# An attention loop of 16 chunks: x loaded as soon as x1 is made, y's high half taken before the second exponentials, x1's low half on GpSimd, and 50 constant products in the tail

## The reference

```
x = x + attention(cond(x, type))        # cond: shared + typed gated FFN, mixed by a gate
x = x + ffn(cond2(x, type))             # cond2: 3 shared + 2 typed FFNs, gated; ffn: router + top-2 of 8 experts
```

```
q, k, v = x @ Wq.T + bq, x @ Wk.T + bk, x @ Wv.T + bv
scores  = einsum('bhqd,bhkd->bhqk', q, k) / sqrt(16), masked above the diagonal
out     = softmax(scores) @ v @ Wo.T + bo
```

## Time and profile before

| what | value |
|---|---|
| time, median of 3 runs | 2447.77 us (2443.02 to 2448.24) |
| the profiled execution's own time | 2434.09 us |
| its span | 2432.5 us |
| PE busy | 2328.6 us, 96% of the span, 18946 matmuls |
| DVE busy | 1164.1 us, 48% |
| ACT busy | 1067.4 us, 44% |
| POOL busy | 294.1 us, 12% |
| attention stage, in the trace | from 573.6 us (constant products ahead of it) to 846.45 us (first L785 of es[0]) |

### The profile page before, as it was taken

How to read it: one execution, slowest core, us unless ns; L and a number is a source line. 1 busy time by engine, 2 the same in 40 slices (tenths; PEclk the granted TensorE clock), 3 DMA queues, 4 the chain that set the end, 5 groups by cost and what they waited for, 6 DMA issues and landing times.

```text
span 2432.5 us, 51603 instructions
## 1 busy us (share of the span) xinstructions
PE 2328.6 (96%) x18946; PEld 1516.3 (62%) x18965; DVE 1164.1 (48%) x2341; ACT 1067.4 (44%) x2049; POOL 294.1 (12%) x466
## 2 busy tenths in 40 slices
PE   5999999997999799999999999999999999989997
PEld 2444588885878544444444788888544444457886
DVE  5554355444888543233232444445344444444444
ACT  3553355442666443233232344433344454446662
POOL 0000000002433000000000111111000000004556
PEclk9999999998999899999999999999999999999999
DMA  3231011001334222021010233343111111002434
GB/s 122 88 100 55 27 53 52 35 14 53 84 91 92 63 104 78 26 78 61 27 61 26 92 117 108 107 140 106 57 38 50 34 35 34 35 35 70 130 96 124
DMA packets 165292, 170.22 MB, mean 70 GB/s; under 512 B 98932, under 2 KB 143348, under 8 KB 156164
## 3 DMA queue, kind: packets, MB, share of 16 engines
q1 hardware_dynamic: 139300, 80.35, 11.3%
q0 software_dynamic: 20720, 72.47, 8.8%
q10 hardware_dynamic: 5104, 15.12, 2.0%
HBM read 107.57 MB, written 50.86 MB: 65 GB/s over the span
## 4 chain that ended last, share of the span: by engine, by line
PE 85%; ACT 4%; SPq 3%; DVE 3%; issue 2%; DMA 2%; POOL 1%; DVEq 0%; POOLq 0%; ACTq 0%
PE ps L767 31%; PE ps L785 25%; PE ps L1042 14%; PE ps L1161 4%; PE ps L1173 4%; PE ps L1031 3%; SPq L508 1%; DMA arena<-in_x 1%; SPq L507 1%; ACT misc L1352 1%; ACT arena L1351 1%; SPq L603 1%; PE ps L1056 1%; PE ps L870 0%; DVE xh L1980 0%
## 5 line engine op out<-in xcount | busy, mean ns | idle before, releaser
L767 PE MATMUL ps<-xh,arena 128*128 (+1 forms) x5376 | 892.7, 308 | 18.4 <-DVE xh L1606 10.2
L785 PE MATMUL ps<-misc,arena 128*128 128x256 f16 (+2 forms) x4128 | 716.1, 309 | 13.8 <-DVE misc L1797 8.0
L767 PEld LDWEIGHTS ps<-xh,arena 128*128 (+1 forms) x5376 | 515.9, 98 | 292.0 <-issue 27.4
L785 PEld LDWEIGHTS ps<-misc,arena 128*128 (+1 forms) x4128 | 393.7, 98 | 231.7 <-issue 12.9
L1801 DVE SCALAR_TENSOR_TENSOR misc<-ps,misc 128x256 f16<-128x256 f32 (+1 forms) x464 | 248.1, 535 | 492.9 <-ACT misc L1273 491.1
L1273 ACT ACTIVATE misc<-ps 128x256 f16<-128x256 f32 (+1 forms) x464 | 218.5, 471 | 525.6 <-PE ps L767 525.6
L1042 PE MATMUL ps<-arena 128*128 128x512 f16 x1536 | 337.2, 379 | 0.0
L1042 PEld LDWEIGHTS ps<-arena 128*128 128x128 f16 x1536 | 148.0, 98 | 172.8
L2059 DVE TENSOR_TENSOR arena<-misc,arena 128x512 f16<-128x512 f32 x128 | 88.6, 692 | 228.5 <-ACT arena L1412 228.3
L1795 DVE TENSOR_TENSOR arena<-ps,misc 128x256 f32<-128x256 f32 (+1 forms) x200 | 101.8, 509 | 146.8 <-ACT misc L1269 146.0
L1411 ACT ACTIVATE misc<-ps,bias 128x512 f32<-128x512 f32 x128 | 87.7, 685 | 173.0 <-PE ps L1042 162.8
(11 more groups left out here) (284 smaller groups left out, 2110.0 us busy)
## 6 DMA issues: line engine op xcount, KB each, us to landing
wstage<-in_m_w POOLq DMA_DIRECT2D x16, 1024.0 KB, 5.9
parts_d<-misc POOLq DMA_DIRECT2D x64, 256.0 KB, 2.5
arena<-src_d SPq DMA_DIRECT2D x64, 256.0 KB, 3.8
src_d<-misc SPq DMA_DIRECT2D x24, 512.0 KB, 3.1
arena<-parts_d ACTq DMA_DIRECT2D x12, 1024.0 KB, 8.2
wstage<-in_c_wi POOLq DMA_DIRECT2D x6, 1024.0 KB, 5.7
wstage<-in_r_w POOLq DMA_DIRECT2D x5, 1024.0 KB, 5.3
cshare_d<-misc SPq DMA_DIRECT2D x8, 512.0 KB, 3.1
```

The costliest lines, as they stand in the source:

```text
L767: last = mm(ps[:, bank, col + c0:col + c0 + width], weight(off, half, g, wp, k * F + f * 128), xh[:, xp, k, ds(start, width)], start=(k == ...
L785: last = mm(ps[:, 4 + 2 * half + m, c0:c0 + width], weight(off, half, 2 if p.gated else 1, wp, f * D + m * 128), hid[:, st % 4, hp, c0:c0 ...
```

## The change

Four edits in the attention and one in the tail:

1. ACT calls `y_high(i + 2)` after the copy of the denominators and ahead of `exponentials(i, 1)`, instead of last in the turn.
2. ACT writes x1 scaled by SX in float32 into a new buffer `x1_scaled` (a part of `misc` that the attention leaves free), and then x1's high part as before.
3. POOL, not DVE, makes x1's low part (`x1_low`), as x1_scaled - high part, last in its turn. ACT waits for POOL's previous one before it overwrites `x1_scaled`, and once more behind the loop for the last one.
4. SP issues `xin_load(i - 1)` ahead of `x1_store(i - 2)`; the load now waits for x1 of the chunk before (`s["x1"]`), and the store waits for x1 and no more for its low part.
5. `keep_clock(2, 38)` becomes `keep_clock(2, 50)`.

```diff
+        x1_scaled = misc[:, 512:1024].rearrange("p (k n) -> p k n", k=KC)
...
-            for i in range(NA + 1):
-                if i >= 1:
+            def x1_low(c):
+                pool.wait_ge(s["x1_hi"], c + 1)
+                cols = ds(c * CH, CH)
+                nc.gpsimd.tensor_tensor(xh[:, 1, :, cols], x1_scaled, xh[:, 0, :, cols], ALU.subtract
+                                        ).then_inc(s["x1_lo"], 1)
+
+            for i in range(NA + 2):
+                if 1 <= i <= NA:
                     normalisers_wide(i - 1)
                 if i + 2 < NA:
                     y_sum(i + 2)
                     y_low(i + 2)
+                if i >= 2:
+                    x1_low(i - 2)
...
             def xin_load(c):
+                if c >= 1:
+                    sp.wait_ge(s["x1"], c)
                 for j in range(GB):
                     load_x(xin[:, :, j * S:(j + 1) * S], c * GB + j).then_inc(s["xin_in"], 16)
 
             def x1_store(c):
-                sp.wait_ge(s["x1_lo"], c + 1)
+                sp.wait_ge(s["x1"], c + 1)
...
+                if 0 <= i - 1 < NA:
+                    xin_load(i - 1)
                 if 0 <= i - 2:
                     x1_store(i - 2)
-                if 0 <= i - 1 < NA:
-                    xin_load(i - 1)
...
-            keep_clock(2, 38)
+            keep_clock(2, 50)
...
+                if i + 2 < NA:
+                    y_high(i + 2)
                 if 0 <= i < NA:
                     exponentials(i, 1)
                 if 0 <= i - 2 < NA:
                     act.wait_ge(s["x1"], i - 1)
+                    if i >= 3:
+                        act.wait_ge(s["x1_lo"], i - 2)
+                    fn(x1_scaled, x1, ACT.Copy, scale=SX)
                     fn(xh[:, 0, :, ds((i - 2) * CH, CH)], x1, ACT.Copy, scale=SX).then_inc(s["x1_hi"], 1)
-                if i + 2 < NA:
-                    y_high(i + 2)
-
+
+            act.wait_ge(s["x1_lo"], NA)
...
-                if 0 <= i - 2 < NA:
-                    dve.wait_ge(s["x1_hi"], i - 1)
-                    cols = ds((i - 2) * CH, CH)
-                    v.scalar_tensor_tensor(xh[:, 1, :, cols], x1, SX, xh[:, 0, :, cols],
-                                           ALU.mult, ALU.subtract).then_inc(s["x1_lo"], 1)
```

## The result

| | before | changed |
|---|---|---|
| time, median | 2448.01 us (2443.02 to 2449.20, 4 runs) | 2414.37 us (2409.48 to 2418.10, 4 runs) |
| ratio | | 0.9865 [0.9841, 0.9889] |
| profiled execution's own time | 2434.09 us | 2409.48 us |
| its span and mean granted clock | 2432.5 us, 0.989 | 2407.9 us, 0.991 |

The change makes the kernel 1.35% faster, 33.6 us between the medians. Between the two profiled executions, whose own times the sum was made from, the difference is 24.6 us where the sum said 20.3. So two things are to be found: what in the traces is larger than forecast, and why the medians lie 9 us further apart than the traces.

A forecast was written before the change was run, and what follows sets the result against it. PE and DVE were taken as nearly full, with PE's floor at 13.5 us per turn. Turns -13.4, loop's end -7.1 and constants +0.2 gave -20.3 us; against 2447.8 the forecast was 2427.5 us, range 2419.0 to 2438.5.

The forecast's parts named there:

- the sum: Whole kernel: turns -13.4, loop's end -7.1, constant products +0.2, together -20.3 us, from 2434.1 to 2413.8 for the profiled execution.
- the step from the sum to the forecast: Whole kernel: the profiled execution lay 13.7 us under the median; against 2447.8 us the forecast is 2427.5.
- They can keep no clock that was not kept: Tail: 12 more constant products before the combination keep no further clock and cost up to 0.3, +0.2 us.
- The turns: Attention's steady turns: from 14.53 to 13.5 us, 1.03 saved in each of 13 turns, -13.4 us.
- the floor: Attention: PE's own work per turn, 13.44 us measured in one turn and rounded up to 13.5.
- Rival B: Attention: DVE and POOL take turns at the shared ports; turns of 14.0, 2434 us, chance 0.16.
- rivals C and D: Attention: C, ACT becomes the ring, 2438.5 us, chance 0.11; D, SP's queue is slower, 2463 us, chance 0.03.
- DVE would fall to 11.5 per turn: Attention: without x1's low part DVE's list falls from 13.16 to 11.5 us at best, so it is no bound.
- The price that the prediction named for this case: Attention, y's high half moved: second exponentials end later; if exponentials began as late as now, PE would wait 0.4 us per turn.
- the longer path behind x1: Loop's end: one more copy and ACT's wait for POOL before es[0] give 1.9 us back.
- The loop's end: From the last turns to es[0]: last x1 9.0 us sooner, less 1.9, -7.1 us, from -3 to -10.
- its lower bound (the clock): Loop's end: -10 us if PE, at 1.2 GHz there, stays at 2.4 GHz.

The follow-up runs named there:

- experiment 2: The changed kernel with 38 constant products instead of 50: 2420.07 us, ratio 0.9918 to the kernel before.
- experiment 4: The kernel before with only SP's edit (load of x ahead of the store, both behind x1), 38 constants: 2426.18 us, ratio 0.9935.
- experiment 7: The kernel before with SP's edit and y's high half moved, x1's low part left on DVE, 38 constants: 2420.38 us, ratio 0.9916.
- experiment 6: The kernel before with only y's high half moved ahead of the second exponentials, 38 constants: 2447.06 us, ratio 1.0023.
- experiment 5: The changed kernel measured once more, no edit: 2416.03 us, ratio 0.9904 to the kernel before.
- experiment 3: The kernel before with 50 constant products instead of 38, nothing else: 2437.85 us, ratio 0.9991.
- experiment 8: The changed kernel without SP's edit (store waits for x1's low part, load behind it): 2462.23 us, ratio 1.0089 to the kernel before.
- experiment 11: The changed kernel with x1's low part left on DVE, 50 constants: 2415.34 us, ratio 0.9892 to the kernel before.
- experiment 10: The changed kernel with two buffers for x and constant products in PE's waits at the loop's end: 2409.13 us, ratio 0.9867 to the kernel before.

## Why the prediction was right or wrong

**The step that failed** is the one from the sum to the forecast: "Against 2447.8 the forecast is 2427.5". It took the 20.3 us from an execution of 2434.09 and moved them to the median of three runs, 13.7 us higher, as if the same offset would stand between the changed kernel's trace and its median. It did not: there the offset was 4.9 us (2409.48 to 2414.37). Of the 13.1 us by which the forecast missed, 8.8 are this difference of the offsets and 4.3 lie in the traces (24.6 against 20.3): the loop's end gave 1.1 more than forecast, the step behind it 1.6 and the first turns 1.6, and the sum had no term for the last two. The offset should have been a question: what in this kernel can differ by 10 us between two executions?

**One cause of the offset was a term of the sum**: "They can keep no clock that was not kept", +0.2 us. It was read from one execution, whose combination ran at 2.4 GHz behind an idle time of 2.34. In 31 of the 71 executions of the kernel before the mean clock was low; in the four traces of kernels with 38 constants where it was 0.985 or less, the combination had fallen to 1.2 GHz and cost 9.3 us more (experiments 2, 4, 7 and, with the same 10.40 behind 2.35 of idle time, 6). At that share the 12 constants are worth 31/71 x 9.3 = 4.1 us on the mean, less 0.3; with the 7.7 between the medians of the two heaps it is 3.4, less 0.3. Experiment 2 against 5 gives 2420.07 - 2416.03 = 4.0 us, but on two chips, and the direct comparison, experiment 3, can't tell 3 or 4 us from none. That the constants keep the clock is shown; what that is worth on the mean is an estimate.

**The rest of the offset was the draw.** The first four runs of before all lie, by their times, in the upper heap (2443.02 and more), and their median of 2448.0 is 8.8 above that of the 71. If the 71 stand for them, four such runs are unlikely by chance alone (26 of the 71 reach 2443.02), so the chip or the hour of the first measurement may have added to it; that stays open, as no clocks are listed for them but the profiled execution's. Without this draw the sum would have done well: the lower heap, for which it was made, has a median of 2436.9, and 2436.9 - 20.3 = 2416.6, where the changed kernel's 10 executions have 2416.0. Some of this closeness is luck, since it leaves out what the constants gain in the other executions, and since the profiled executions lie 2.8 and 6.5 us below these medians.

**The turns: right in the mechanism, and in the number by two small errors that cancel.** Forecast 1.03 per turn, 13.4 in all; the traces give 13.2. A turn of before was 14.42 on the mean of the 13, and not the 14.53 of seven of them (two of the first were 13.56). And the floor is lower: a turn without pauses is 13.26 (686.74 to 700.00, and 703.57 to 716.83 in experiment 7), not 13.5; the mean of the 13 is 13.40. The difference of 1.8 us over 13 turns is what is left of three longer turns, of 14.45, 14.11 and 13.61, each with a pause of PE (below), and a shorter first one of 12.68. Rival B's contention was real, but POOL is the one that pays; rivals C and D did not come about. That DVE would fall to 11.5 per turn was right (11.6).

**The credit for the turns: partly wrong.** The prediction gave ACT's wait for x to SP's edit and PE's 1.2 us to y's high half, as two separate gains. They are one. The ring of x (load and landing 7.06, bias, exponentials, x1's high and low part, store, load) set the turn, and y's high half, last in ACT's list, was late because ACT's list was. SP's edit alone brings a turn of 14.42 to 13.55 (experiment 4; 14.1 was expected). Then y's high half is the next limit, and moving it gives the last 0.3. Moved alone it gives nothing, and lengthens a turn from 14.42 to 14.81 on the mean (experiment 6), since it delays the second exponentials, which hang on x. The price that the prediction named for this case ("the cover would be gone and PE would wait 0.4 per turn") is what happened, but larger: PE waited 11.2 us in 10 turns there, in place of its former wait for POOL, and the turn became 0.4 longer. Experiment 8 bears the ring out: with one copy more, y's high half and POOL's low part in it, a turn is 16.0, where 16.1 was expected. So the parts do not add: 0.9935 and 1.0023 apart, 0.9916 together.

**x1's low part on POOL: wrong in its use in the turns, right in its price at the end.** In the turns it was to relieve DVE, which needed no relief: experiments 7 and 11 reach 13.26 with this work still on DVE. At the end the prediction charged 1.9 us for the longer path behind x1, and the traces show it: 4.60 us from the last x1 to L796, where it is 2.83 before (843.62 to 846.45) and 2.82 in experiments 7 and 11. It shows in no total because the last x1 itself comes some 1.8 us sooner than with the low part on DVE (25.7 us behind chunk 14's denominators, against 27.7 and 27.5).

**The loop's end: -7.1 forecast, -8.2 in the traces, and 1.6 more** behind L785, which the forecast had only as its lower bound (the clock). The last x1 was to come 9.0 us sooner and came 9.9 sooner (48.92 behind the 13 turns before, 38.98 now), less 1.8 for the path behind it. The clock was not kept there (0.76 in the window, as before), but was back before L796. That is not so in every execution: in experiment 5's trace the same L796 took 2.72 instead of 1.46. This is a part of what two executions of the changed kernel differ by: of the 5.3 us between these two traces 2.2 have come together by the first L796, and 1.5 arise in the step behind it. Experiment 10 shows what keeping it is worth: 3.5 us in the traces on top of two buffers (28.4 to 24.9), 2.2 between the medians.

Still open: why the executions of the kernel before divide as 40 to 31 and not otherwise, why the first four all lay in the upper heap, and what else makes the differences within a heap (some 3 to 4 us to either side). No run here was made for that.

## What to carry to other kernels

Before several waits are removed one by one, follow the longest ring of the stage (here load, bias, exponentials, x1, store, load) and cut that first: a wait elsewhere may be its shadow, and moving work ahead within the ring can make it longer. Where one profiled execution stands well off the median, don't carry the offset over to the changed kernel, but look for an idle time of TensorE just ahead of dense products, and compare times by their listed clocks. Constant products that fill such an idle time to its end can be worth more on the mean than a single trace shows: 0.3 us of cost in the trace here, and an estimated 3 to 4 us of gain on the mean.

## What the runs showed of the hardware

- An idle time of 2.2 to 2.35 us before 384 short products was followed by 2.4 GHz in two traces and 1.2 GHz in four, of kernels that differ only elsewhere; by the mean clocks the kernel before alone has both (31 of 71 at 0.985 or less, and 49 of 99 with the other kernels of 38 constants). With 4.73 us five of six executions were at 0.985 or less; without idle time none of 34 was, experiment 8 left out. Once at 1.2 GHz, TensorE stayed there for the whole combination, 20.5 us in which the profile shows it busy all the time, with products of 64 columns.
- In the middle of groups that wait for nothing, PE pauses. The first of these two pauses stands at the same line in every trace with turns of 13.26, as 0.38 us (experiment 10) to 1.21 us (experiment 2); the kernel before has one elsewhere (1.50 us ahead of L883 at 736.05), and experiments 6 and 8 have none above 0.4 us from 600 to 800. PE's timeline of the changed kernel:

```profile
657.87 0.33 PE L898 MATMUL ps<-arena 128*128 128x128 f16 x3 [1.02 <-issue]
...
670.95 0.80 PE L975 MATMUL ps<-arena 128*64 128x128 f16 x21 [0.60 <-issue]
```

- These pauses of 1.0 and 0.6 us, put down to issue, are most of the 2.4 us for which PE is idle in the 13 turns (the rest is 0.56 of waiting for ACT at 617.49 and a third pause of 0.19). What causes them was not tried.
